# Layer-0 attention of a four-stage kernel: order of TensorE's work in a slot, whole-half reciprocals, and a layernorm cut finer over three pairs

## The reference

```
q, k, v = x @ w_q, x @ w_k, x @ w_v          # 16 heads of 64
dot = (q/8) . (k/8), causal mask; att = softmax(dot)
out = (att . v).reshape(b, n, 1024) @ w_u + b_u
```

## Time and profile before

| | |
|---|---|
| median of 3 runs | 2856.82 us (2853.74 to 2860.49) |
| the profiled execution | 2854.86 us, span 2853.1 us |
| busy over the span: PE, VectorE (DVE), ScalarE (ACT), GpSimd (POOL) | 2379.2, 1542.7, 1264.2, 845.3 us |
| POOL L298, adds of probabilities, 320 | 550.7 us |
| DVE L596, reciprocals of 128x128, 256 | 228.2 us, mean 924 ns |
| DVE L573, maxima over 128x1024, 128 | 156.7 us, mean 1225 ns |
| ACT L487, L503, copies of 128x512 (projection, output) | mean 598 ns |
| POOL L89, inverse root of the variances, in attention | mean 1648 ns |
| PE L443, values times ring tiles, 1280 | 249.8 us, 38.2 us idle before them |

### The profile page before, as it was taken

How to read it: one execution, slowest core, us unless ns; L and a number is a source line. 1 busy time by engine, 2 the same in 40 slices (tenths; PEclk the granted TensorE clock), 3 DMA queues, 4 the chain that set the end, 5 groups by cost and what they waited for, 6 DMA issues and landing times. The chain is left out here.

```text
span 2853.1 us, 42941 instructions
## 1 busy us (share of the span) xinstructions
PE 2379.2 (83%) x15692; PEld 1436.2 (50%) x15692; DVE 1542.7 (54%) x3484; ACT 1264.2 (44%) x1756; POOL 845.3 (30%) x756
## 2 busy tenths in 40 slices
PE   5999989998999899569999947888888588846687
PEld 3555554555455554358888833343333244424464
DVE  3676677667765767345666653223230355446534
ACT  2554445444544444113333215757577355523341
POOL 1667656765676577300000010000000101010000
PEclk9999999999999999759999968889899798978889
DMA  2000000000000000100000000000000000020001
GB/s 64 1 1 1 1 1 1 1 1 1 1 1 1 1 1 1 39 18 0 0 0 0 0 3 1 1 1 1 0 0 1 3 1 1 0 69 0 0 1 30
DMA packets 35355, 17.88 MB, mean 6 GB/s; under 512 B 15226, under 2 KB 33028, under 8 KB 35204
## 3 DMA queue, kind: packets, MB, share of 16 engines
q1 hardware_dynamic: 35204, 15.86, 2.2%
HBM read 13.76 MB, written 2.10 MB: 6 GB/s over the span
## 5 line engine op out<-in xcount | busy, mean ns | idle before, releaser
L298 POOL TENSOR_TENSOR a_first<-a_first,a_ring 128x1024 f32<-128x1024 f32 (+3 forms) x320 | 550.7, 1721 | 235.7 <-ACT a_ring L521 196.9
L521 ACT ACTIVATE a_ring<-a_st 128x768 f32<-128x768 f32 (+1 forms) x256 | 234.7, 917 | 286.5 <-PE a_st L428 286.5
L1517 ACT ACTIVATE g_probsT<-g_s_ps 128x1024 f32<-128x1024 f32 (+2 forms) x320 | 282.9, 940 | 152.6 <-PE g_s_ps L1344 144.4
L443 PE MATMUL a_o_ps<-a_ring,a_v 128*64 128x512 f32 (+3 forms) x1280 | 249.8, 484 | 38.2 <-POOL a_ring L285 38.2
L596 DVE RECIPROCAL a_row_inv<-a_row_inv 128x128 f32<-128x128 f32 x256 | 228.2, 924 | 18.4 <-ACT a_row_inv L509 18.4
L573 DVE TENSOR_REDUCE a_part_max<-a_mx 128x2 f32<-128x1024 f32 x128 | 156.7, 1225 | 123.8 <-PE a_mx L399 123.8
L948 PE MATMUL m_up<-m_xT_hi,m_w_hl 128*128 x640 | 211.8, 402 | 7.1 <-DVE m_glu L997 4.3
L981 ACT ACTIVATE m_silu<-m_up,m_bias 128x512 f32<-128x512 f32 x160 | 110.1, 688 | 238.8 <-PE m_up L948 238.8
L1338 PE MATMUL g_s_ps<-g_qT,g_kT 64*128 64x512 f32 (+2 forms) x640 | 156.9, 492 | 36.0 <-ACT g_probsT L1517 29.8
L1366 PE MATMUL g_o_ps<-g_probsT,g_values 128*32 128x512 f32 (+3 forms) x1536 | 170.8, 535 | 17.3 <-ACT g_probsT L1517 15.7
L580 DVE CUSTOM_DVE_ANT_0 a_masked<-a_mx,mask_wide 128x256 bf16<-128x256 f32 (+3 forms) x256 | 112.8, 487 | 110.0 <-PE a_mx L399 109.9
(11 more groups left out here) (339 smaller groups left out, 4473.4 us busy)
## 6 DMA issues: line engine op xcount, KB each, us to landing
m_w<-in_L_ffn_rw SPq DMA_DIRECT2D x2, 1024.0 KB, 8.7
s_w<-in_L_ffn_w SPq DMA_DIRECT2D x1, 2048.0 KB, 10.9
s_w<-in_L_ffn_w SPq DMA_DIRECT2D x4, 512.0 KB, 10.7
out_x<-x SPq DMA_DIRECT2D x4, 512.0 KB, 3.2
m_w<-in_L_ffn_rw SPq DMA_DIRECT2D x2, 512.0 KB, 7.7
x<-in_L_attn_x SPq DMA_DIRECT2D x1, 512.0 KB, 3.5
a_outT<-in_L_attn_w_q SPq DMA_DIRECT2D x1, 512.0 KB, 4.4
a_outT<-in_L_attn_w_k SPq DMA_DIRECT2D x1, 512.0 KB, 6.0
```

What stands on the lines that cost most here:

```text
L298: pool.tensor_tensor(total[:, :, q:q + w], total[:, :, q:q + w], probs_of(n, u)[:, :, off:off + w], ALU.add).then_inc(added, 1)
L443: last = pe.matmul(o_ps[rows_of(h), first_q:first_q + w], v_half[n // 4 % 2][:, j, head:head + A_HD], probs_of(n, u)[:, h, off:off + w], s ...
L521: act.activation(probs_of(n, u)[:, :, 0:w], st_ps[u % 2][:, :, 0:w], ACT.Exp).then_inc(exp_done, 1)
L1517: act.activation(out, src.rearrange("p k (j n) -> p k j n", j=at_once), ACT.Exp, scale=float(HD) ** -0.5).then_inc(exp_done, 1)
```

## The change

1. On TensorE, `weigh` goes from its place behind the early maxima to a place behind the side work, in front of the late maxima.
2. The reciprocals of a half of the row sums are one instruction on 512 columns, in slot 2 (first half of the pair before) and slot 5 (second half), in place of four quarters over the slots 2, 5, 6, 7 and 9. `inv_ready` counts one for a half.
3. Normalising pieces hold two blocks in place of four (`fine=True`). The layernorm of the batch before is spread over the second and third pair of a batch (`FINISHING`), that of the next input over the third and fourth (`NORMALIZING`). GpSimd's inverse root moves to u = 7 of the second pair and u = 3 of the fourth.

```diff
--- before.py
+++ after.py
@@ -46,7 +46,7 @@
 NORM_STEPS = 2 * NB + 5
 
 
-def layernorm_parts(dve, chain, x_of, out_of, t, count):
+def layernorm_parts(dve, chain, x_of, out_of, t, count, fine=False):
 
 
 
@@ -73,9 +73,9 @@
             chain.did(dve.tensor_scalar(out_of(blk), x_of(blk), t.mean[:, blk:blk + 1], t.rstd[:, blk:blk + 1],
                                         ALU.subtract, ALU.mult))
 
-    quarters = [range(blk, blk + 2) for blk in range(0, NB, 2)]
+    halves, quarters = ([range(blk, blk + n) for blk in range(0, NB, n)] for n in (4, 2))
     return [*(lambda q=q: statistics(q) for q in quarters), variance,
-            *(lambda q=q: normalize(q) for q in (range(0, 4), range(4, NB))), chain.settle]
+            *(lambda q=q: normalize(q) for q in (halves, quarters)[fine]), chain.settle]
 
 
 def layernorm(*args):
@@ -130,7 +130,9 @@
 MAXES_EARLY = {0: (0, 7), 3: (1, 0), 6: (1, 3), 7: (1, 4), 8: (1, 5), 9: (1, 6)}
 MAXES_LATE = {0: (0, 8), 1: (0, 9), 3: (1, 1), 4: (1, 2)}
 PROJECTIONS = {0: 0, 1: 1, 3: 2, 4: 3}
-INVERSES = {2: (1, 0, 2, 4), 5: (1, 1, 0, 3), 6: (1, 1, 3, 4), 7: (0, 0, 0, 1), 9: (0, 0, 1, 2)}
+INVERSES = {2: 0, 5: 1}
+FINISHING = {1: {2: (0, 1), 4: (1, 3), 5: (3, 4), 6: (4, 5)}, 2: {2: (5, 6), 4: (6, 7), 5: (7, 8), 6: (8, 9), 7: (9, 10)}}
+NORMALIZING = {2: {8: (0, 2), 9: (2, 4)}, 3: {2: (4, 5), 4: (5, 7), 5: (7, 8), 6: (8, 10)}}
 OUT_SLOTS = PAIRS + 1
 XN_CHAIN = [NORM_STEPS * (b + 1) + (NORM_STEPS + 1) * max(0, b - 1) for b in range(BATCH)]
 
@@ -301,7 +303,7 @@
                 def scale_output(n, c):
                     out = outT[:, n % OUT_SLOTS, c * HALF:(c + 1) * HALF]
                     pool.wait_ge(o_kept, 2 * n + c + 1)
-                    pool.wait_ge(inv_ready, 4 * (2 * n + c + 1))
+                    pool.wait_ge(inv_ready, 2 * n + c + 1)
                     pool.tensor_tensor(out, out, row_inv[c][:], ALU.mult).then_inc(out_kept, 1)
 
                 normed = 1
@@ -314,7 +316,8 @@
                         cut_diagonals(n, u)
                         if u not in FIRST_OF_CHUNK:
                             add_up(n, u)
-                        if u == 4 and (n % PAIRS == 2 and n // PAIRS + 1 < BATCH or n % PAIRS == 1 and n > PAIRS):
+                        if (u == 3 and n % PAIRS == 3 and n // PAIRS + 1 < BATCH
+                                or u == 7 and n % PAIRS == 1 and n > PAIRS):
                             inverse_root(pool, norm, g.minus_half[:, 0:NB], normed)
                             normed += 1
                 for c in range(2):
@@ -455,10 +458,6 @@
                             score(n, s)
                         for of, k in maxima_of_slot(n, MAXES_EARLY, s):
                             maxima(of, k)
-                        if running and s > 0:
-                            weigh(n, s - 1)
-                        elif n > 0 and s == 0:
-                            weigh(n - 1, UNITS_A_PAIR - 1)
                         if n > 0 and s == 2:
                             add_rows(n - 1, 1)
                         if running and s == 2:
@@ -475,6 +474,10 @@
                             turn_input(b, c)
                         for b, t in outputs_of_slot(n, s):
                             output(b, t)
+                        if running and s > 0:
+                            weigh(n, s - 1)
+                        elif n > 0 and s == 0:
+                            weigh(n - 1, UNITS_A_PAIR - 1)
                         for of, k in maxima_of_slot(n, MAXES_LATE, s):
                             maxima(of, k)
 
@@ -590,10 +593,9 @@
                     found = largest[:, 4 * c:4 * c + 4, :].unsqueeze(3)
                     dve.tensor_reduce(out, found, AX.X, ALU.max).then_inc(max_ready, 1)
 
-                def invert_sums(n, c, quarter):
-                    cols = slice(quarter * P, (quarter + 1) * P)
+                def invert_sums(n, c):
                     dve.wait_ge(sums_kept, 2 * n + c + 1)
-                    dve.reciprocal(row_inv[c][:, cols], row_inv[c][:, cols]).then_inc(inv_ready, 1)
+                    dve.reciprocal(row_inv[c][:], row_inv[c][:]).then_inc(inv_ready, 1)
 
                 def add_bias(b, t):
                     dve.wait_ge(y_done, 4 * b + t + 1)
@@ -605,7 +607,7 @@
                 def normalized(b, count):
                     dve.wait_ge(x_loaded, 3 * 16)
                     return layernorm_parts(dve, chain, lambda blk: g.x[:, b * NB + blk, :],
-                                           lambda blk: x_norm[:, blk, :], norm, count)
+                                           lambda blk: x_norm[:, blk, :], norm, count, True)
 
                 def finished(b, count):
 
@@ -617,7 +619,7 @@
                         chain.did(dve.tensor_tensor(x_all, x_all, y[:], ALU.add))
                         chain.settle()
 
-                    parts = layernorm_parts(dve, chain, y_of, y_of, norm, count)[:-1] + [residual]
+                    parts = layernorm_parts(dve, chain, y_of, y_of, norm, count, True)[:-1] + [residual]
                     first_part = parts[0]
 
                     def when_kept():
@@ -626,22 +628,25 @@
 
                     return [when_kept] + parts[1:]
 
-                def pieces_of(n):
-
-                    count = 1 + n // PAIRS * 2
-                    if n >= 0 and n % PAIRS == 2 and n // PAIRS + 1 < BATCH:
-                        return normalized(n // PAIRS + 1, count)
-                    if n > PAIRS and n % PAIRS == 1:
-                        return finished(n // PAIRS - 1, count - 1)
-                    return []
-
-                PIECES_BEFORE = (0, 0, 1, 4, 5, 5, 5, 5, 6, 6)
+                finishing = {b: finished(b, 2 * b + 2) for b in range(BATCH - 1)}
+                normalizing = {b: normalized(b, 2 * b - 1) for b in range(1, BATCH)}
+
+                def pieces_of_slot(n, s):
+
+                    b, pair = divmod(n, PAIRS)
+                    pieces = []
+                    if n > 0 and b >= 1 and s in FINISHING.get(pair, {}):
+                        start, stop = FINISHING[pair][s]
+                        pieces += finishing[b - 1][start:stop]
+                    if n > 0 and b + 1 < BATCH and s in NORMALIZING.get(pair, {}):
+                        start, stop = NORMALIZING[pair][s]
+                        pieces += normalizing[b + 1][start:stop]
+                    return pieces
 
                 for c in range(2):
                     low_input(0, c)
                 for n in range(-1, ALL_PAIRS + 1):
                     running, m = 0 <= n < ALL_PAIRS, n + 1
-                    pieces = pieces_of(n)
                     for s in range(UNITS_A_PAIR):
                         for of, k in maxima_of_slot(n, MAXES_EARLY, s):
                             read_maxima(of, k)
@@ -657,11 +662,9 @@
                             low_input(b, c)
                         for b, t in outputs_of_slot(n, s):
                             add_bias(b, t)
-                        if s in INVERSES:
-                            back, c, start, stop = INVERSES[s]
-                            for quarter in range(start, stop) if 0 <= n - back < ALL_PAIRS else ():
-                                invert_sums(n - back, c, quarter)
-                        for piece in pieces[PIECES_BEFORE[s]:PIECES_BEFORE[s + 1] if s < 9 else len(pieces)]:
+                        if s in INVERSES and 0 <= n - 1 < ALL_PAIRS:
+                            invert_sums(n - 1, INVERSES[s])
+                        for piece in pieces_of_slot(n, s):
                             piece()
                 for part in finished(BATCH - 1, 2 * BATCH - 1):
                     part()
```

## The result

| | before | changed |
|---|---|---|
| median | 2855.28 us (4 runs) | 2954.37 us (2945.07 to 2959.45, 4 runs) |
| ratio | | 1.0343, 95% interval 1.0322 to 1.0365 |
| profiled span | 2853.1 us | 2950.2 us |
| reciprocals | 256, mean 924 ns | 64, mean 3342 ns |

The change makes the kernel 3.4% slower, 98 us (92 to 104). The forecast was 2949, in the range 2912 to 2975. The ratios of this document leave out two executions in a slow state, one of the kernel before (5784.29 us) and one of `e9_pieces_bunched` (3086.47 us).

What follows compares the result with a forecast made beforehand. TensorE was taken as the bound, busy 1004.41 of 1083.37 us in attention. Terms 82 - 3 + 3 + 0 + 10 = +92 on the profiled 2854.86 gave 2946.9; with the median 2 above, 2949 us, range 2912 to 2975.

Steps and rivals of the forecast that it cites:

- Part A: Weigh behind the side work uncovers VectorE's latency: +2.64 us a pair over 31 pairs, +82 us.
- the terms: Wait changes per pair: slot 1 +1.08, slot 2 +0.73, slot 4 +0.89, slot 5 +0.54, slot 0 -0.60 us.
- The three output pairs: In three pairs, slot 7's output projections lose a weigh before their wait for GpSimd's scaled outputs: +3 us.
- Part B: One reciprocal for a half, in slots 2 and 5, hides behind PE's own order of work: 0.
- The room of 0.6 us: In slots 2 and 5 the long reciprocal ends 0.6 us before the next maxima can be read.
- Part C: Layernorm pieces over three pairs: between -13 and +25 us, taken as +10 for late reads and GpSimd's adds.
- the loss end: Layernorm groups of two each meet one GpSimd add, up to 2.08 us: 12 x 2.08 = +25 us.
- PE's busy time "the same": In the profile after, attention's span is some 90 us longer while PE's busy time stays the same.
- The faster rival: Side work in front takes all 38.2 us of cut waits, layernorm spreading gives 13: 2806 us; chance 0.04.

Runs made afterwards that it cites:

- e9_pieces_bunched: Changed kernel with the normalising groups of slots 4, 5 and 6 put together in slot 4; ratio to the kernel before 1.033 (1.028 to 1.038).
- The three runs on slots: Kernel before with weigh behind the side work only in slots 1 and 4, 2 and 5, or 0; ratios 1.0210, 1.0203, 0.9989.
- e1_weigh_only: Kernel before with weigh behind the side work in every slot, reciprocals and layernorm pieces as before; ratio 1.0273, +78 us.

## Why the prediction was right

- *Part A, +82 by the working.* Alone it gave +78 (71 to 85). The four distances from maxima to user came out exactly, and an ordinary pair grew by 2.59 against 2.64. Slot by slot too: from the late maxima of slot 0 to those of slots 1, 3, 4 and the next slot 0 the changed kernel took 1.01, 0.70, 0.87 and 0.02 us longer, where the terms give 1.08, 0.73, 0.89 and 0.54 - 0.60 = -0.06. The pairs of the last batch grew by 1.8, as forecast. The terms don't hold one by one, though: taken alone slot 0 is -0.34 in place of -0.60, as GpSimd's next cut stood behind that wait, and the row sums cost 0.2 more. The three runs on slots give +3.02 a pair together, the whole 2.59.
- *The three output pairs, +3.* Beyond an ordinary pair's growth they gave 1.0, 2.6 and 1.0; 1.6 of the 2.6 are slower matmuls at a granted clock of 0.97.
- *Part B, 0.* +1 (-5 to +6). The room of 0.6 us was there. By the fixed cost of an instruction in the Trainium skill (VectorE: DVE Perf Modes, The TRN2 errata) a half would have saved an estimated 0.18 us; the trace doesn't agree: one instruction took 3.34 us against 3.39 for four back to back, 0.05 less.
- *Part C, +10.* +14 without part A, 18 in the stretch with it. Sign and slots were right (the late read, the group in front of the input transposes, though these are in the fourth pair and not the third, as I wrote; I didn't see that this pair would be the worst), the mechanism only in part. I priced it by waits for GpSimd and late reads at full clock. Behind A and B that is the larger part: VectorE's busy time grew by 17.3 us, where the loss end had 25, and 13.5 of the 18.2 us are standing. Alone part C is all slower matmuls, which I had at nothing.
- *PE's busy time "the same".* It grew by 21.3 us in the changed kernel, 17.2 of it in nine pairs with a granted clock below 1.00, and 16.7 of the 21.3 are there without part C. I had seen a granted clock of 1.00 over waits of up to 2.8 us and left the clock out of the rivals. The waits of the changed kernel are longer (3.63), but those of part A alone are not, and the clock fell there too.
- *Luck in the sum.* The terms give 92 us. The stretch grew by 104.6 and the profiled span by 97.1, since the parts ahead of the stretch and behind it, which the terms hardly touch, were 2.0 and 5.4 us shorter in this execution. The median lies 5 us from the forecast; that is closer than the terms are.
- *The faster rival* was wrong for the reason given with it: VectorE's results are there 2.41 us after the maxima, and score ends at 1.12. Its -38 for cut waits was not to be had by PE's order alone.
- My test "wrong if the pairs that normalise stand out more than the ordinary ones lose" was a poor one: the fourth pair does (+9.3 against +2.6), and still most of the loss is in the ordinary ones, as there are so many.

## What to carry to other kernels

Before independent work is moved in an in-order queue, measure from the last instruction that starts a chain on another engine to the first one that needs its result; if the work in between shrinks below that distance, the difference is paid each time round. A wait that moving removes may only be the first in line: look what the same releasing engine has queued next. Work that is spread finer is not cheaper by itself: here four groups in one place cost the stretch 18 us less than the same groups over three slots in front of reads. And look at the bounding engine's busy time, not only at its waits: its clock can fall behind them.

## What the runs showed of the hardware

- **The clock behind a wait.** In the changed kernel PE waited 3.63 us for maxima, ran one group of maxima and waited 1.66 more; then the granted clock was 0.54. PE's timeline there:

```profile
191.24 0.49 PE L402 MATMUL a_mx<-a_k_hi,a_q_hi 64*128 64x512 f32 x2 [3.63 <-DVE a_part_max L576]
193.39 1.08 PE L364 MATMUL a_p_ps<-ident,a_x_norm 128*128 128x128 f32 x4 [1.66 <-DVE a_x_norm L73]
```

  The windows row of the same pair in e9, where PE waited 2.48 us and no second time, has the clock at 1.00 and 32.15 us busy:

```profile
162.10:199.90 37.80, 32.15 (x212) 17.09 (x210) 27.70 (x60) 17.50 (x24) 25.81 (x24) 1.00 0.00 1
```

  The Trainium skill (TensorE: Matmul & The Clock Gate, What's actually happening) has the clock set by how busy the array has been recently; the trace agrees. A fall of the clock cost some 2 us of slower matmuls beside the waits (busy 34.81 us in the changed kernel's pair, where an ordinary pair's 30.85 and the 1.33 for the transposes, 31.93 less 30.60, make 32.18: 2.6 there, 1.6 to 2.1 in eight other pairs).

  The length of one wait doesn't decide it. With part A alone (`e1_weigh_only`) no wait of PE for maxima is over 1.8 us. PE's timeline and a windows row there, with the clock at 0.74:

```profile
425.51 0.50 PE L399 MATMUL a_mx<-a_k_hi,a_q_hi 64*128 64x512 f32 x2 [1.79 <-DVE a_largest L580]
```

```profile
425.00:429.00 4.00, 3.49 (x17) 1.82 (x17) 3.40 (x9) 0.29 (x1) 3.60 (x5) 0.74 0.00 0
```

  The kernel before has the same wait in the same slot, and a longer one behind it, and its granted clock is 1.00 in every pair:

```profile
400.08 0.50 PE L399 MATMUL a_mx<-a_k_hi,a_q_hi 64*128 64x512 f32 x2 [1.79 <-DVE a_largest L580]
...
407.12 0.50 PE L399 MATMUL a_mx<-a_k_hi,a_q_hi 64*128 64x512 f32 x2 [2.74 <-DVE a_largest L580]
```

  What tips the clock stays open here; each of the other kernels here, the changed one too, has pairs in which it fell.
- **VectorE behind GpSimd's add.** The variance step that took 2.25 us took 0.17 in all six places of the changed kernel, but other steps of the same piece were long in its place: L61 took 1029 ns on average, L63 708, against 164 and 168 before. VectorE's and GpSimd's timelines there:

```profile
422.41 1.95 DVE L61 SCALAR_TENSOR_TENSOR a_norm_square<-a_norm_stats 128x8 f32<-128x8 f32 x1
...
424.37 1.25 DVE L63 TENSOR_TENSOR a_norm_twice<-a_norm_stats 128x8 f32<-128x8 f32 x1
```

```profile
421.94 2.39 POOL L300 TENSOR_TENSOR a_first<-a_first,a_ring 128x1024 f32<-128x1024 f32 x1 [2.44 <-ACT a_ring L524]
424.29 1.30 POOL L307 TENSOR_TENSOR a_outT<-a_outT,a_row_inv 128x512 f32<-128x512 f32 x1
```

  Both steps end within 0.03 us of the GpSimd instruction beside them. In the first batch the normalising groups took 3.19 us for four blocks, 2.34 and 2.14 for two. That the length is a wait for GpSimd is argued from these times; no run took the adds away.
